# A decoder layer on one core: the last head's solve gets PSUM banks, buffers and instruction orders of its own

## The reference, cut to what matters

```python
state = state * exp(g_t)
corr  = einsum('bhk,bhkv->bhv', k_t, state)
v_new = (v_t - corr) * b_t
state = state + einsum('bhk,bhv->bhkv', k_t, v_new)
o_t   = einsum('bhk,bhkv->bhv', q_t, state)      # then norm, * o_norm_w * silu(x @ Wg.T), @ Wo.T, + x
```

## Time and profile before

| | us |
|---|---|
| median of 3 runs | 618.94 (618.31 to 618.95) |
| profiled execution, own time | 617.76 |
| its span, first to last instruction | 616.0 |
| mean granted TensorE clock | 0.961 |

### The profile page before, as it was taken

The page is one execution under the profiler, slowest core; times in us unless marked ns, Lnnn a source line. Parts: engine busy times, 40 slices in busy tenths (PEclk is TensorE's granted clock), DMA queues, the critical chain, the costliest instruction groups (busy, mean ns, idle before and its releaser), DMA issues.

```text
span 616.0 us, 15291 instructions
## 1 busy us (share of the span) xinstructions
PE 558.9 (91%) x6463; PEld 376.4 (61%) x6463; DVE 460.0 (75%) x1091; ACT 356.0 (58%) x555; POOL 26.3 (4%) x36
## 2 busy tenths in 40 slices
PE   3769879999999999999999999999997979758997
PEld 2325336577757675766576667657766857646646
DVE  6577898877979797978788878887795612589663
ACT  0748394588459655946684768458842322277451
POOL 3011000100010001000100100010000000100000
PEclk9979999999999999999999999999997978967999
DMA  5000203101110121021002101110101140000002
GB/s 162 1 0 2 70 9 71 28 1 27 56 27 1 27 58 25 10 65 14 22 14 65 11 20 22 59 28 2 27 11 29 24 150 3 1 0 2 0 1 68
DMA packets 49699, 18.62 MB, mean 30 GB/s; under 512 B 39100, under 2 KB 48352, under 8 KB 49632
## 3 DMA queue, kind: packets, MB, share of 16 engines
q1 hardware_dynamic: 49632, 17.66, 12.1%
HBM read 14.49 MB, written 3.15 MB: 29 GB/s over the span
## 4 chain that ended last, share of the span: by engine, by line
PE 72%; DVE 16%; ACT 8%; issue 2%; DMA 1%; SPq 0%; ACTq 0%; DVEq 0%
PE bank L1167 16%; DVE acc L790 8%; PE bank L1214 6%; PE bank L1340 4%; PE bank L1344 4%; PE bank L1129 4%; PE bank L1431 3%; PE bank L1233 3%; PE bank L1299 3%; PE bank L1356 3%; PE bank L1217 3%; PE bank L1350 3%; PE bank L1352 2%; PE bank L1354 2%; PE bank L1211 2%
## 5 line engine op out<-in xcount | busy, mean ns | idle before, releaser
L790 DVE SCALAR_TENSOR_TENSOR acc<-bank,cw,acc 128x508 f32<-128x508 f32 (+2 forms) x240 | 176.4, 739 | 41.9 <-ACT acc L508 37.6
L1167 PE MATMUL bank<-xnT,wq 128*128 128x512 f32 x320 | 154.8, 610 | 16.2 <-DVE acc L790 15.7
L1167 PEld LDWEIGHTS bank<-xnT,wq 128*128 128x128 f32 x320 | 56.4, 191 | 75.9 <-issue 45.3
L508 ACT ACTIVATE acc<-bank,cw 128x512 f32<-128x512 f32 x80 | 55.5, 694 | 46.9 <-PE bank L1167 46.2
L1214 PE MATMUL bank<-kq 128*128 128x384 f32 x128 | 50.7, 499 | 0.2
L523 ACT ACTIVATE vT<-acc 128x512 f32<-128x512 f32 x32 | 21.3, 673 | 46.1 <-DVE acc L790 46.0
L821 DVE SCALAR_TENSOR_TENSOR AM<-bank,rb,DT 128x384 f32<-128x384 f32 x64 | 37.5, 606 | 1.8 <-PE bank L1214 1.5
L554 ACT ACTIVATE T<-bank 64x512 f32<-64x512 f32 x16 | 9.5, 592 | 44.9 <-PE bank L1233 34.6
L883 DVE SCALAR_TENSOR_TENSOR xres<-bank,f,xres 128x256 f32<-128x256 f32 x64 | 26.9, 478 | 10.3 <-PE bank L1344 10.0
L573 ACT ACTIVATE Yd<-Yc 32x512 f32<-32x512 f32 x32 | 20.1, 628 | 21.3 <-DVE Xc L870 21.0
L523 ACT ACTIVATE kq<-acc 128x512 f32<-128x512 f32 x48 | 31.4, 658 | 1.2 <-DVE acc L790 0.9
(11 more groups left out here) (242 smaller groups left out, 1083.8 us busy)
## 6 DMA issues: line engine op xcount, KB each, us to landing
wq<-in_w_qkv SPq DMA_DIRECT2D x8, 640.0 KB, 4.1
blocks<-AM SPq DMA_DIRECT2D x128, 8.0 KB, 1.6
xres<-in_x SPq DMA_DIRECT2D x2, 512.0 KB, 4.6
Yl<-in_y_init SPq DMA_DIRECT2D x8, 128.0 KB, 2.6
Bl<-blocks SPq DMA_DIRECT2D x8, 128.0 KB, 2.0
wg<-in_w_gate SPq DMA_DIRECT2D x8, 128.0 KB, 2.1
solved<-Yl SPq DMA_DIRECT2D x8, 128.0 KB, 2.4
Yc<-solved SPq DMA_DIRECT2D x64, 16.0 KB, 2.0
```

The lines of the kernel that those rows point to most:

```text
L508: a(acc[:, u % RING, :, :], bank[6 + u % 2][:, :].rearrange("p (b l) -> p b l", b=4), ACT.Copy, scale=cw[:, t, 3:4]).then_inc(s_tap.next(f ...
L790: stt(w, ps[:, :, 0:L - s], cw[:, t, 3 - s:4 - s], w, ALU.mult, ALU.add).then_inc(s_cv.next(f"u{u}_{s}"), 1)
L1167: ins = mm(bank[6 + u % 2][:, :], wq[:, cc, t, :], xnT[:, cc, 512 * half:512 * half + 512], start=cc == 0, stop=cc == KC - 1)
```

## The change

Phases 6 to 8 get tables of their own (NEXT_, LAST_ and FINAL_). The last head's tiles go to a second ring, `tail`, in banks 0 to 2, which are free once vt3 of head 7 has been emptied; so tiles of head 6 and head 7 no longer wait for each other's banks. Where the shared counters had ordered the two heads, `read` and a few explicit waits take their place. Yd is doubled, T32 gets memory of its own (it lay in Xc), and the wait for yd in front of T32 goes. In the last phase SyncE loads wg ahead of the gather and the epilogue's inputs ahead of the scatter. The idle products of the last head go from 4, 8, 20 and 14 to 2, 3, 6 and 8 (mm and my1 keep 5 each).

```diff
+NEXT_SCALAR_ORDER = ("lt' +0 -0 +1 +2 mt0' mt1' -1 w1_0' w1_1' +3 dt0 dt1 w2_0' +4 -2 w2_1' sq0' +5 -3 sq1' -4 rs' q0 +6 "
+                "-5 rt' q1 +7 dt2 cs +8 -6 -7 ga0 nr ga1 +9 -8 ta -9 yd").split()
+LAST_SCALAR_ORDER = ("lt' mt0' mt1' w1_0' w1_1' w2_0' w2_1' sq0' sq1' ga0 ga1 ta rs' rt' lt yd").split()
+FINAL_SCALAR_ORDER = ("mt0' mt1' w1_0' w1_1' w2_0' w2_1' sq0' sq1' rs' rt'").split()
+NEXT_VECTOR_ORDER = ("u u u ly' u u s u s my0' s u s s s u s s s s s my1' s u s s s s s r2_0' s u u u s r2_1' s s s s s u "
+                "s u u on0' u s u on1' u ms' s s u rf' s wo0' wo1' u u u wo2' s wo3' u u rb e1_0 e1_1 e2_0 e1_2 e1_3 "
+                "e2_1 e1_4 e1_5 e2_2 e1_6 e1_7 u u xa e2_3 u u u u tb xc rq vt0 vt1 vt2 vt3").split()
+LAST_VECTOR_ORDER = ("s s s s s s s s s s s s s ly' s s s s s s s s s s s s s s s s s my0' my1' r2_0' r2_1' xa on0' on1' "
+                "tb xc ms' ly rf' wo0' wo1' wo2' wo3'").split()
+NEXT_TENSOR_ORDER = ("0 ly' 1 2 mt0' dt0 mm' dt1 my1' w1_0' w1_1' 3 r2_0' r2_1' 4 w2_0' 5 w2_1' o0' o1' dt2 sa' rs' 6 rn' "
+                "wo0' ca wo1' 7 wo2' cs wo3' ga0 nrm e1_0 e1_1 8 e2_0 e1_2 e1_3 e2_1 e1_4 e1_5 e2_2 e1_6 e1_7 e2_3 "
+                "ga1 9 ta tb vt0 vt1 vt2 vt3").split()
+LAST_TENSOR_ORDER = ("lt' ga0 ly' ga1 mt0' mm' my1' w1_0' w1_1' r2_0' r2_1' w2_0' w2_1' o0' o1' ta sa' rs' tb rn' wo0' lt "
+                "ly wo1' wo2' mt0 wo3' mm").split()
+FINAL_TENSOR_ORDER = ("my1' w1_0' w1_1' r2_0' r2_1' w2_0' w2_1' o0' o1' sa' rs' rn' wo0' wo1' wo2' wo3'").split()
-IDLE = {"tb": 4, "lt": 8, "ly": 20, "mt0": 14, "mm": 5, "my1": 5}
+IDLE = {"tb": 2, "lt": 3, "ly": 6, "mt0": 8, "mm": 5, "my1": 5}
...
-        Yd = sb("Yd", [P, CH, P])
+        Yds = [sb(f"Yd{i}", [P, CH, P]) for i in range(2)]
-        T32 = Xc
+        T32 = sb("T32", [P, CH, BLK])
...
+        tail = Ring(bank[0:3], SOLVE, sem("last_solve_tile_filled"), {...}, origin=H - 1, credit=0)
+        def solving(h):
+            return tail if h == H - 1 else post
+        def read(engine, h, name):
+            if h == H - 1:
+                engine.wait_ge(post.fills.sem, post.fills.at(name, h - 1))
...
+                if last:
+                    sp.wait_ge(post.fills.sem, post.fills.at("ga1", h - 1))
+                    load_gate(h)
                 gather(h, par)
-                if not first:
-                    sp.wait_ge(post.fills.sem, post.fills.at("ga1", h - 1))
-                load_gate(h)
-                scatter(h, not last)
                 if last:
                     load_epilogue()
+                else:
+                    if not first:
+                        sp.wait_ge(post.fills.sem, post.fills.at("ga1", h - 1))
+                    load_gate(h)
+                scatter(h, not last)
...
                 if name[:2] == "ga":
-                    take(name, h, gate[:, bs, :], ACT.Silu).then_inc(post.emptied(name).next(name), 1)
+                    if h == H - 1 and k == 0:
+                        act.wait_ge(post.emptied("o1").sem, post.emptied("o1").at("o1", h - 1))
+                    take(name, h, gate[:, bs, :], ACT.Silu).then_inc(ring.emptied(name).next(name), 1)
...
                 elif name == "lt":
-                    act.wait_ge(s_yd.sem, s_yd.at("yd", h))
+                    read(act, h, "ly")
...
+                if ring is tail and ago:
+                    pe.wait_ge(prep.emptied("vt3").sem, prep.emptied("vt3").at("vt3", H - 1))
+                    return ring.tile(name)
```

More of the change, by code:

```diff
@@ new lines @@
+FINAL_VECTOR_ORDER = ("my0' my1' r2_0' r2_1' on0' on1' ms' rf' wo0' wo1' wo2' wo3'").split()
+NEXT_TENSOR_ORDER = ("0 ly' 1 2 mt0' dt0 mm' dt1 my1' w1_0' w1_1' 3 r2_0' r2_1' 4 w2_0' 5 w2_1' o0' o1' dt2 sa' rs' 6 rn' "
[3 more added lines that the diff above has]
+                "ly wo1' wo2' mt0 wo3' mm").split()
@@ L436, in _ @@
             g = nc.gpsimd
-            g.memset(Yd[:, :, :], 0.0)
+            for placed in Yds:
+                g.memset(placed[:, :, :], 0.0)
             g.memset(Xd[:, :, :], 0.0)
@@ L462, in _ @@
                 g.tensor_tensor(Yc[:, :, SUB:BLK], T16[:, :, SUB:BLK], T16[:, :, SUB:BLK], ALU.add).then_inc(s_z.next("z"), 1)
-            pool.wait_ge(post.fills.sem, post.fills.at("wo3", H - 1))
+            pool.wait_ge(tail.fills.sem, tail.fills.at("wo3", H - 1))
             g.tensor_copy(identb[:, :], ident)
@@ L551, in take @@
             def take(name, h, dst, func, rows=slice(0, P), split=4):
-                act.wait_ge(post.fills.sem, post.fills.at(name, h))
-                return a(dst, post.tile(name)[rows, :].rearrange("p (b d) -> p b d", b=split), func)
+                ring = solving(h)
+                act.wait_ge(ring.fills.sem, ring.fills.at(name, h))
+                return a(dst, ring.tile(name)[rows, :].rearrange("p (b d) -> p b d", b=split), func)
             def solve_step(name, h):
@@ L587, in solve_step @@
                 elif name == "rs":
-                    act.wait_ge(post.fills.sem, post.fills.at(name, h))
-                    a(osum[:, :], post.tile(name)[:, 0:P], ACT.Copy).then_inc(post.emptied(name).next(name), 1)
+                    read(act, h, "rn")
+                    act.wait_ge(ring.fills.sem, ring.fills.at(name, h))
+                    a(osum[:, :], ring.tile(name)[:, 0:P], ACT.Copy).then_inc(ring.emptied(name).next(name), 1)
             def phase(h, old, now, new):
@@ L593, in phase @@
                     act.wait_ge(s_cw.sem, s_cw.at("cw", h + 1))
-                for step in SCALAR_ORDER if old or now else FIRST_SCALAR_ORDER:
+                for step in {-1: FIRST_SCALAR_ORDER, H - 2: NEXT_SCALAR_ORDER, H - 1: LAST_SCALAR_ORDER, H: FINAL_SCALAR_ORDER}.get(h, SCALAR_ORDER):
                     if step[0] == "+":
@@ L858, in solve_step @@
                 bs = slice(4 * k, 4 * k + 4)
+                ring, Yd = solving(h), Yds[h % 2]
                 if name[:2] in ("tb", "ly", "my", "r2", "wo"):
-                    dve.wait_ge(post.fills.sem, post.fills.at(name, h))
-                    done = post.emptied(name).next(name)
+                    dve.wait_ge(ring.fills.sem, ring.fills.at(name, h))
+                    done = ring.emptied(name).next(name)
                 if name == "xa":
+                    read(dve, h, "lt")
+                    if h == H - 1:
+                        dve.wait_ge(s_yd.sem, s_yd.at("yd", h - 1))
                     dve.wait_ge(s_yc.sem, s_yc.at(str(NB - 1), h))
@@ L908, in phase @@
                 rounds = [(f, k) for k in range(SUB - 1) for f in (substitute, subtract)] if now else []
-                for step in VECTOR_ORDER if old or now else FIRST_VECTOR_ORDER:
+                for step in {-1: FIRST_VECTOR_ORDER, H - 2: NEXT_VECTOR_ORDER, H - 1: LAST_VECTOR_ORDER, H: FINAL_VECTOR_ORDER}.get(h, VECTOR_ORDER):
                     if step == "s":
@@ L1291, in solve_step @@
                     made("o1", h)
-                ps = post.tile(name) if name == "rs" else fill(post, {"sa": "rs", "mm": "mt1"}.get(name, name), h)
+                ps = ring.tile(name) if name == "rs" else fill(ring, {"sa": "rs", "mm": "mt1"}.get(name, name), h)
                 if name in ("ta", "tb"):
@@ L1324, in solve_step @@
                         merge_t(ps, par, 8 + c)
[L1325 to L1327 removed]
+                        ins = merge_y(py, Yd, c)
+                    ring.fills.next("mt1")
+                    ins.then_inc(ring.fills.next("my0"), 2)
                     return
@@ L1358, in solve_step @@
                 if name != "sa":
-                    ins.then_inc(post.fills.next(name), 1)
+                    ins.then_inc(ring.fills.next(name), 1)
             def phase(h, par, old, now, new):
-                for step in TENSOR_ORDER if old or now else FIRST_TENSOR_ORDER:
+                for step in {-1: FIRST_TENSOR_ORDER, H - 2: NEXT_TENSOR_ORDER, H - 1: LAST_TENSOR_ORDER, H: FINAL_TENSOR_ORDER}.get(h, TENSOR_ORDER):
                     if step.isdigit():
```

78 lines of the change are left out of this document (45 added, 33 removed).

## The result

The changed kernel takes 611.26 us (median of 10 runs, 609.30 to 616.64) against 619.02 for the kernel before on the same chip (10 runs, 618.31 to 620.04). The ratio is 0.9883, 95% interval 0.9856 to 0.9911: faster by 1.2%, 0.96 us above the forecast of 610.3 and inside its range. The profiled execution took 609.89 us, span 608.1, mean granted clock 0.966. One run of the kernel before in the later set of e8, e9 and v2 took 1252.52 us; it counts in no ratio here.

What follows compares the result with a forecast made beforehand. Bound: TensorE's chain of waits behind the seventh head, with the solve late behind SyncE's block issues. 8.82 - 0.7 + 0.46 = 8.6 us off 617.76 gives 609.2 profiled, median 610.3; range 605.5 to 616.

Steps and rivals of the forecast that it cites:

- Part 1: Phase 6 in the new order: the gather starts at 457.9 instead of 461.5, 3.6 us earlier.
- Part 2: Merges of head 6: mt0' starts 6.65 us later at 475.5, yet ta of head 7 comes 2.25 us earlier at 493.45.
- the clock will be low at mt0' as it was before, so the merges keep their 17.94 us: Merges of head 6, up to the end of o1': low clock again, so they end at 493.45.
- the better case: Rival: the merges of head 6 find the clock high, 3 us better, 607 and below; chance 0.06.
- Part 3: From ta to mt0 of head 7: 12.6 us plus 1.0 for stops instead of 20.2; mt0 at 507.05, 8.82 us earlier.
- I had charged 1.0: TensorE's instruction stops behind ta of head 7: 1.0 us kept of the former 4.36, bounds 0 and 4.36.
- that assumes full clock and no unexplained stop: Condition on the 12.6 us summed step by step from ta to mt0 of head 7.
- clock, in part: Rival: the clock falls near tb of head 7 and returns before the merges, 5 us back, 615; chance 0.13.
- the loads end before solved: Epilogue's loads, now issued at 468.6 to 470.3, are done at 478.9, before solved at 479.4; cost 0.
- Part 4: From mt0 of head 7 to the epilogue: +0.7 us before mm, -0.46 us at the last root.
- the 0.7 us forecast: mt0 to mm of head 7: wo3' and 5 idle products now stand between them, +0.7 us.
- the 0.46 us charged for it: Last root: without the table load in front of it VectorE goes on 0.46 us earlier.

Runs made afterwards that it cites:

- e8: Changed kernel with projection 9 of head 7 moved between ta and tb of head 6; median 612.59 us, ratio 0.9891 to the kernel before.
- e9: Changed kernel with mt0 of head 7 issued between wo1' and wo2' instead of behind both; median 613.62 us, ratio 0.9897 to the kernel before.
- v2: Changed kernel with idle products 10 (tb), 8 (ly), 3 (mt0), 5 (my1), projection 9 between ta and tb, ly' after 7 solve steps; 610.49 us, ratio 0.9849.
- v1: Changed kernel with idle products 10 before tb, 8 before ly, 3 before mt0, 5 before my1, none before lt and mm; 609.17 us, again 610.25.
- e5: Kernel before with only the epilogue's loads moved ahead of the last head's scatter; median 616.38 us, ratio 0.9951 to the kernel before.
- e2: Changed kernel with T32 copied behind the six yd copies on ScalarE, as before; median 614.68 us, ratio 0.9927 to the kernel before.
- e6: Kernel before with the new orders in phase 6 alone, its own orders after it; median 625.05 us, ratio 1.0087 to the kernel before.
- e7: Changed kernel with wg issued behind the gather instead of ahead of it; median 614.73 us, ratio 0.9915 to the kernel before.
- e4: Changed kernel with no idle products in the last head; median 614.36 us, ratio 0.9905 to the kernel before.
- e1: Changed kernel with the epilogue's loads back behind the scatter; median 613.89 us, ratio 0.9919 to the kernel before.

## Why the prediction was right

Part 1 held: first block 457.70 (forecast 457.9), with wg's issue in front of it and ga1's end setting it; first solve step 469.85 (470.2).

Part 2 held in its order and missed the clock. mt0' came at 476.2, not 475.5, and 0.5 of the difference had come about before phase 6. A new wait lies in it all the same: VectorE waited 1.09 us for ly of head 6, since TensorE had stopped for 1.33 us in tb and then run its transposes and ga0 at 0.50; counted from the first projection of head 7, the first solve step came 0.9 us earlier than forecast, which made up for most of it. The failing step is "the clock will be low at mt0' as it was before, so the merges keep their 17.94 us". It was low earlier, until 472.8, and the merges took 14.3. I had the better case as a rival at 3 us with 0.06; in the 11 traces of the new orders it came 6 times, so it deserved about half.

Part 3, the order of events, held: ta directly behind o1', T16 begun 2.5 us behind ta's start and done at 2.9 (forecast: begun at 2.9), yd beside ly. TensorE stopped for 0.13 us in tb and for 0.98 in lt, and I had charged 1.0; the 0.47 us of "issue" at 492.12 in the chain are no stop of TensorE, but lie between ScalarE's two gate copies. The failing step is "that assumes full clock and no unexplained stop" (12.6 us): the clock fell at 500.1, ly took 1.97 us where I had 1.2, wo1' and wo2' 3.71 where I had 1.7, the idle products 1.35 where I had 1.0. That is 3.1 of the 3.2 us between 16.8 and 13.6. The rival "clock, in part" is what happened there (priced at 5 us, it cost about 3). The three traces with v1's counts, at full clock, have 13.8 to 13.9 us; their idle products are other ones, but they bear out the 13.6 forecast for a full clock. That the loads end before solved was right as well (477.3 and 480.2), and the longer hop from solved to Yc cost nothing, as ta waits for o1'; but xa ended only 0.8 us before ta, not 5.

Part 4: mt0 to the epilogue 22.16 against 21.7. mt0 to mm grew by the 0.7 us forecast. The table load before the last root is gone, but the 0.46 us charged for it did not come: from mm to the epilogue it is 19.46 us after and 19.44 before.

So the sum of 8.6 us for the profiled execution came out as 7.87 (617.76 less 609.89), because +3.2 in ta to mt0, +0.7 at mt0' and +0.5 behind it stood against -3.6 in the merges. The direction was right, and the traces show the gain at the places that the forecast named; the agreement to 1 us is luck in part, since errors of over 3 us cancelled.

The spread has grown: on the chip of the result the kernel before ran within 1.7 us, the changed one within 7.3; on other chips the kernel before spread too, up to 616.2 to 624.8 (without the run of 1252.52). Over the 78 runs of the versions with the new orders, time goes with the time spent at clock 0.50 (worked out as twice one minus the mean clock, times the span): correlation 0.85, slope 0.34 us per us. What decides whether the clock falls near 479 stays open; near 500 the idle products have a part in it, as the table shows, but e9 escaped the fall with the changed kernel's counts.

## What to carry to other kernels

Before moving an early producer forward, follow who waits for its result last: here the gather was early for nothing as long as the consumers' chain was not cleared (625.05 alone, 611.26 together; that chain cleared alone was not run). Compare two traces from a mark ahead of the edit, not from the start of the span: in e8 that turns 2.1 us into 0.15. When a stretch consists of small tiles, make the forecast at both levels of the clock and give each a chance near one half, since the same program took 14.3 and 17.5 us for it. Judge a place for idle products by several executions: one trace said 606.8, the median of its 12 runs 609.2.

## What the runs showed of the hardware

- TensorE's stops for instructions follow the q8 queue. It went on 2.3 to 2.7 us after the next q8 transfer had begun: transfer at 497.74 and on at 500.33, 501.53 and 503.88 in the kernel before, 461.03 and 463.38 after, 499.9 and 502.23 in e5. In each of the 13 traces with two or more such stops the TensorE records between their ends are a multiple of 256: 256 between 500.33 and 503.88 in the kernel before, 1280 between 463.38 and 497.88 after. So the stops come where one piece of instructions ends. In the 14 traces no two of these transfers began less than 3.2 us apart, while ta or tb runs through 128 products in 1.3 us. That this is why there are stops with no load near them is an inference from these figures.
- From the issue of solved to the first Yc it was 1.7 to 1.9 us in six traces (before, e2, e5, e6, e7, v2) and 3.2 to 4.0 in the other eight, with large loads ahead in e2, e7, after and e4 and none in e1. It is the write itself that has two values: solved landed 1.7 to 1.8 us after its issue in the six and 3.2 to 3.9 in the eight. Why stays open.
- In e7 the granted clock stayed at 0.50 for 13.6 us from 500.6, and TensorE was busy for 13.36 of them (window below); in the earlier trace rows it was 11.2 of 13.6.

```profile
500.60:514.20 13.60, 13.36 (x296) 10.69 (x295) 4.83 (x12) 5.91 (x10) 0.00 (x0) 0.50 0.02 4
```
